# Chunk 1's token halves in a buffer of their own, and three engines' instruction order around the end of the front

## The reference

```
x = x + gated_delta(layernorm(x), Wq, Wk, Wv, Wo, Wb, bb, Wd, bd)
x = x + ffn(layernorm(x), w1, w2, w3)

gated_delta: q, k, v = x Wq, x Wk, x Wv;  beta = sigmoid(x Wb + bb);  delta = softplus(x Wd + bd)
             S_t = beta_t * S_{t-1} + delta_t * (k_t outer v_t);  o_t = q_t S_t;  out = o Wo
ffn:         quantize(w) = clip(round(w / (mean|w| + 1e-8)), -1, 1)
             (sigmoid(x q(w1)^T) * (x q(w2)^T)) q(w3)^T
```

## Time and profile before

| | us |
|---|---|
| median of 3 runs (341.34 to 343.6) | 341.43 |
| the profiled execution | 342.33 |
| its span, first to last instruction | 340.6 |
| TensorE busy in the span | 331.5 |
| VectorE, ScalarE, GpSimd busy | 205.7, 141.2, 102.0 |

### The profile page before, as it was taken

How to read it: one execution, slowest core, us unless ns; L and a number is a source line. 1 busy time by engine, 2 the same in 40 slices (tenths; PEclk the granted TensorE clock), 3 DMA queues, 4 the chain that set the end, 5 groups by cost and what they waited for, 6 DMA issues and landing times.

```text
span 340.6 us, 5194 instructions
## 1 busy us (share of the span) xinstructions
PE 331.5 (97%) x1824; PEld 184.4 (54%) x1824; DVE 205.7 (60%) x454; ACT 141.2 (41%) x270; POOL 102.0 (30%) x350
## 2 busy tenths in 40 slices
PE   8999999979999999999999999999999999999996
PEld 6888878864544544445455444454554444444442
DVE  3777999489978967276388652564886412343411
ACT  1588767789673663322324250223242102323200
POOL 5797645586001105990011044600110300000000
PEclk9999999999999999999999999999999999999999
DMA  7999700474572351400004022000030320000011
GB/s 204 365 387 403 280 0 2 92 95 94 102 115 47 50 106 41 115 32 2 0 0 64 0 70 86 31 1 3 0 62 2 73 81 33 0 0 3 0 62 62
DMA packets 45658, 26.94 MB, mean 79 GB/s; under 512 B 37568, under 2 KB 38080, under 8 KB 45632
## 3 DMA queue, kind: packets, MB, share of 16 engines
q1 hardware_dynamic: 45312, 26.62, 29.2%
q10 hardware_dynamic: 320, 0.00, 0.0%
HBM read 13.89 MB, written 4.19 MB: 53 GB/s over the span
## 4 chain that ended last, share of the span: by engine, by line
PE 83%; POOL 7%; DVE 4%; issue 3%; DMA 1%; ACT 1%; SPq 0%; POOLq 0%
PE ffn L1060 45%; PE ffn L1074 22%; PE lev L955 4%; PE lev L985 4%; PE ffn L924 2%; PE oc L971 2%; DMA w_nat<-xs 1%; POOL rs L377 1%; PE oc L968 1%; DVE X L742 1%; PE lev L974 1%; POOL xs L440 1%; PE oc L958 1%; DVE stats L680 1%; PE oc L960 1%
## 5 line engine op out<-in xcount | busy, mean ns | idle before, releaser
L1060 PE MATMUL ffn<-w_nat,w12T 128*128 128x512 f16 x704 | 155.3, 379 | 2.5 <-DMA w_nat<-xs 2.5
L1060 PEld LDWEIGHTS ffn<-w_nat,w12T 128*128 128x128 f16 x704 | 68.6, 98 | 84.6 <-issue 2.7
L1074 PE MATMUL ffn<-w3T,w_nat 128*128 128x512 f16 x352 | 76.6, 379 | 0.0
L644 ACT ACTIVATE xnT<-ffn 128x512 f32<-128x512 f32 x44 | 26.2, 596 | 99.4 <-PE ffn L1060 99.3
L871 DVE SCALAR_TENSOR_TENSOR xnT<-ffn,xnT 128x512 f32<-128x512 f32 x44 | 30.3, 689 | 57.1 <-PE ffn L1060 56.9
L1074 PEld LDWEIGHTS ffn<-w3T,w_nat 128*128 128x128 f16 x352 | 34.4, 98 | 42.6 <-ACT w_nat L650 1.0
L376 POOL TENSOR_TENSOR ve<-mv,rconst 128x2 f32<-128x2 f32 x16 | 3.3, 206 | 127.2 <-DVE mv L684 127.2
L885 DVE SCALAR_TENSOR_TENSOR x_sb<-ffn,x_sb 128x512 f32<-128x512 f32 x16 | 11.1, 691 | 43.1 <-PE ffn L1074 43.1
L876 DVE TENSOR_TENSOR w_nat<-xnT,w_nat 128x512 f16<-128x512 f32 x44 | 30.9, 701 | 0.4
L650 ACT ACTIVATE w_nat<-xnT 128x512 f16<-128x512 f32 x44 | 27.4, 623 | 6.5 <-DVE xnT L871 6.4
L680 DVE BATCH_NORM_STATS2 stats<-x_sb 128x6 f32<-128x512 f32 x32 | 20.5, 683 | 2.2 <-issue 1.8
(11 more groups left out here) (118 smaller groups left out, 375.5 us busy)
## 6 DMA issues: line engine op xcount, KB each, us to landing
x_sb<-in_L_attn_x_dram SPq DMA_DIRECT2D x16, 256.0 KB, 8.2
out_dram<-x_sb SPq DMA_DIRECT2D x16, 256.0 KB, 2.0
w_nat<-in_L_ffn_w_dram SPq DMA_DIRECT2D x2, 1536.0 KB, 12.5
w_nat<-in_L_ffn_w_dram SPq DMA_DIRECT2D x2, 1408.0 KB, 14.5
w_nat<-in_L_ffn_w_dram SPq DMA_DIRECT2D x2, 1280.0 KB, 13.3
wv<-in_L_attn_Wv_dram SPq DMA_DIRECT2D x1, 256.0 KB, 5.1
wo<-in_L_attn_Wo_dram SPq DMA_DIRECT2D x1, 256.0 KB, 12.9
w_nat<-xs SPq DMA_TRANSPOSE x16, 3.3
```

Source lines behind the costliest of these rows:

```text
L644: nc.scalar.activation(sig[:, u % 2, :], bank[2 * u % 3][:, :], ACT.Sigmoid, scale=1.0 / XS).then_inc(sig_ready, 1)
L1060: done = nc.tensor.matmul(bank[n % 3][:, :], w12T[:, a * DT + t, u * P:(u + 1) * P], xT[:, g, part, t, :], start=t == 0 and part == 0, sto ...
L1074: done = nc.tensor.matmul(bank[(2 * HT + m) % 3][:, :], hid[:, part, j, m * P:(m + 1) * P], w3T[:, j, :], start=part == 0 and j == 0, stop ...
```

## The change

Chunk 1, and every later odd chunk, writes its fp16 halves into `xs_odd`, which lies over slot 0 of `xn`. That slot is last read by the transposes of chunk 6 (`tile_T` 14), and its front part is used by `q3` in group 0. So the waits are altered: `xhi(1)` waits for `tile_T` 14 where it waited for chunk 0's transposes, chunks 2 and up wait for the transposes of chunk c-2, `sign3(0)` waits for chunk 1's transposes, and `xhi(3)` waits for all transposes of the third weight. Then instructions are moved:

- GpSimd: the mask of level 0 is made behind `fetch(0)` and no longer ahead of `gates(0)` (a new semaphore `masks_made` tells VectorE); `norm(4)` stands ahead of `gates(1)`; `xlo(0)` ahead of `norm2(1)`.
- ScalarE: `apply(6)` ahead of `xhi(0)`, `vcopy(5)` ahead of `sign12(0)`, and `xhi(1)` ahead of `apply(7)`.
- VectorE: `chain1(0)` ahead of `gates(1)`; `apply(6)` ahead of `steps(0)`; `round12(0)` behind `mean_var(7)` and `xlo(0)`; `round12(1)` behind `xlo(1)`; `steps(1)` in unit 1 of group 0 where it was in unit 2.
- TensorE: `spread(1)` after unit 0 of group 0, where it was after unit 1. Nothing else moves on TensorE. SP's order is as before.

```diff
+        xs_odd = xn[:, 0, :, :].rearrange("p b d -> p (b d)").bitcast(f16).rearrange("p (b s d) -> p b s d", b=B, s=2)
...
+        def halves(c):
+            return xs_odd if c % 2 else xs
...
-                    sp_.dma_start_transpose(xT_tile(c, b), xs[:, b, :, :].rearrange("p s n -> p (s n)")
+                    sp_.dma_start_transpose(xT_tile(c, b), halves(c)[:, b, :, :].rearrange("p s n -> p (s n)")
...
             def xlo(c):
-                if c > 0:
-                    pool.wait_ge(xT_in, 16 * B * c)
+                if c > 1:
+                    pool.wait_ge(xT_in, 16 * B * (c - 1))
                 pool.wait_ge(xhi_ready, B * c + 1)
-                nc.gpsimd.tensor_tensor(xs[:, 0, 1, :], xn2[:, 0, :], xs[:, 0, 0, :],
+                nc.gpsimd.tensor_tensor(halves(c)[:, 0, 1, :], xn2[:, 0, :], halves(c)[:, 0, 0, :],
...
-            make_masks(range(1))
             gates(0)
             fetch(0)
+            make_masks(range(1))
+            norm(4)
             gates(1)
-            norm(4)
             fetch(1)
             gates(2)
             norm(5)
             norm2(0)
             norm(6)
+            xlo(0)
             norm2(1)
-            xlo(0)
             norm(7)
             xlo(1)
...
             def sign3(j):
                 act.wait_ge(rounded3, DT if j < 5 else 2 * DT)
+                if j == 0:
+                    act.wait_ge(xT_in, 16 * B * 2)
...
                 if s == "xhi":
-                    if c > 0:
-                        act.wait_ge(xT_in, 16 * B * c)
+                    if c > 1:
+                        act.wait_ge(xT_in, 16 * B * (c - 1))
+                    if c == 1:
+                        act.wait_ge(tile_T, 2 * 7)
+                    if c == 3:
+                        for n in range(QS):
+                            act.wait_ge(w3_in[n], 16 * len(range(n, HT, QS)))
                     for b in range(B):
                         act.wait_ge(xn2_ready, B * c + b + 1)
-                        nc.scalar.activation(xs[:, b, 0, :], xn2[:, b, :], ACT.Copy).then_inc(xhi_ready, 1)
+                        nc.scalar.activation(halves(c)[:, b, 0, :], xn2[:, b, :], ACT.Copy).then_inc(xhi_ready, 1)
...
+            apply(6)
             attn("xhi", 0)
-            apply(6)
             zcopy(5)
             evacuate_T(6)
+            vcopy(5)
             sign12(0)
-            vcopy(5)
+            attn("xhi", 1)
             apply(7)
             zcopy(6)
             evacuate_T(7)
-            attn("xhi", 1)
             sign12(1)
...
             attn("chain0", 0)
+            attn("chain1", 0)
             gates(1)
-            attn("chain1", 0)
...
+            apply(6)
             steps(0)
-            apply(6)
             attn("norm2", 1)
-            round12(0)
             mean_var(7)
             attn("xlo", 0)
+            round12(0)
             attn("apply", 1)
-            round12(1)
             apply(7)
             attn("xlo", 1)
+            round12(1)
             gates(3)
...
-                        if u == 2:
+                        if u == 1:
                             steps(1)
...
-                    if g == 0 and u == 1:
+                    if g == 0 and u == 0:
                         spread(1)
```

More of the change, by code:

```diff
@@ L126, in build_gated_delta_ternary_ffn @@
         bias_in = sem("bias_in")
-        consts, filled = sem("consts"), sem("filled")
+        consts, filled, masks_made = sem("consts"), sem("filled"), sem("masks_made")
         resid_ready = sem("resid_ready")
@@ L369, in make_masks @@
                                                      pattern=[[-2 * h, n], [0, h]], channel_multiplier=1))
-                    nc.gpsimd.affine_select(out=m, in_=m, compare_op=ALU.is_gt, fill=0.0, base=h,
-                                            pattern=[[2 * h, n], [0, h]], channel_multiplier=-1)
+                    made = nc.gpsimd.affine_select(out=m, in_=m, compare_op=ALU.is_gt, fill=0.0, base=h,
+                                                   pattern=[[2 * h, n], [0, h]], channel_multiplier=-1)
+                made.then_inc(masks_made, 1)
             def rstd(c, n, mv, rs, scale, after=None):
@@ L761, in attn @@
                     dve.wait_ge(levels_done, c + 1)
-                    if c > 0:
+                    if c == 0:
+                        dve.wait_ge(masks_made, 3)
+                    else:
                         dve.wait_ge(o_done, c)
@@ L799, in attn @@
                 if s == "xlo":
-                    if c > 0:
-                        dve.wait_ge(xT_in, 16 * B * c)
+                    if c > 1:
+                        dve.wait_ge(xT_in, 16 * B * (c - 1))
                     dve.wait_ge(xhi_ready, B * c + 2)
-                    nc.vector.tensor_tensor(xs[:, 1, 1, :], xn2[:, 1, :], xs[:, 1, 0, :],
+                    nc.vector.tensor_tensor(halves(c)[:, 1, 1, :], xn2[:, 1, :], halves(c)[:, 1, 0, :],
                                             ALU.subtract).then_inc(xlo1_ready, 1)
```

## The result

The changed kernel takes 339.29 us (median of 7 runs, 339.15 to 339.53) against 341.48 for the kernel before beside it. The ratio on record is 0.992, with a 95% interval of 0.9896 to 0.9944. The medians differ by 2.2 us or 0.64%, where 3.3 us were forecast (338.1). It is inside the stated range of 337.6 to 340.2, and inside "within 1%", the likeliest case. Between the two profiled executions the span fell by 2.8 us, from 340.6 to 337.8. How 2.8 in the traces and 2.2 in the medians go together is the first thing the experiments had to settle.

A forecast was written before the change was run, and what follows sets the result against it. TensorE was taken as the bound, busy 331.5 of 340.6 us. Levels 0.73, chunk 7 0.0, group 0 2.53 and its start 0.0 gave 3.3 us: 338.1 from the 341.43 median, range 337.6 to 340.2.

The forecast's parts named there:

- within 1%: Outcome class for the whole kernel: time changes by no more than one per cent, 3.4 us; chance 0.60.
- three named waits of TensorE in the front: TensorE waits before chunk 0's levels (0.73), chunk 7's transposes (0.30) and group 0 (2.53), together 3.56 us.
- second rival: Chunk 7's transposes: `xhi(1)` holds `apply(7)` back, TensorE begins at 65.2 to 65.8; total 338.5 to 339.1; chance 0.13.
- Wait three: Before group 0, TensorE waits for chunk 1's transposed halves; all 2.53 us go, with 1.9 us to spare.
- Wait one: Before chunk 0's levels, TensorE waits for VectorE's chain; the wait goes whole, 0.73 us.
- I cost it at nothing: `norm(4)` ahead of `gates(1)` on GpSimd costs nothing; with `fetch(1)` late, at most 0.73 us would be lost.
- Wait two: Before chunk 7's transposes, TensorE's wait stays at about 0.3 us (0 to 0.5), starting at 64.8.
- The port rule: GpSimd and certain VectorE instructions exclude each other; TensorE would begin chunk 7's transposes at 65.0, sum 3.1 instead of 3.3.
- the quiet 4.67: GpSimd's two root chains before `norm(7)` ends: 4.67 us, costed from a chain in quieter company, against 5.46 before.
- The new buffer is what lets `xhi(1)` stand in front: ScalarE, before group 0: `xhi(1)` can move ahead because it no longer waits for chunk 0's halves to leave `xs`.
- the slower rival: Group 0: `spread(1)` stalls TensorE if `xlo(1)` ends after 67.1; later units lose 1.5 or more; 341.7 to 343; chance 0.05.

The follow-up runs named there:

- mask_early: The changed kernel with the level-0 mask made first of all on GpSimd, no longer behind `fetch(0)`; 339.05 us, ratio 0.9891.
- one_buffer: The changed kernel with all its orders, but every chunk's halves in `xs` again, with the waits of before; 339.32 us, ratio 0.99.
- move_one: The kernel before with only ScalarE's `xhi(1)` moved ahead of `apply(7)`, in the one buffer; 344.24 us, ratio 1.0054.
- chain_only: The kernel before with only the edits around chunk 0's chain (level-0 mask, `norm(4)`, `chain1(0)` ahead of `gates(1)`); 341.29 us, ratio 0.9971.
- xhi1_late: The changed kernel with ScalarE's `xhi(1)` back behind `apply(7)`, `zcopy(6)` and `evacuate_T(7)`; 342.94 us, ratio 1.0035.
- spread_late: The changed kernel with `spread(1)` after unit 1 and `steps(1)` in unit 2 again, as before; 339.38 us, ratio 0.9912.
- both: The changed kernel with the level-0 mask made first on GpSimd, and chunk 7's statistics, `norm(7)` and `apply(7)` moved forward; 338.79 us, ratio 0.9895.
- move_two: The kernel before with ScalarE's `xhi(1)` ahead of `apply(7)` and the second buffer with its waits; 339.75 us, ratio 0.9929.

## Why the prediction was right, and where its terms were off

The forecast's case came true: three named waits of TensorE in the front were the whole matter, nothing behind group 0's start moved (264.40 us both times), and no rival decided. (TensorE began chunk 7's transposes at 65.35, inside the 65.2 to 65.8 of the second rival, but `apply(7)` waited for `norm(7)` and not for `xhi(1)`, which ended at 63.75.) The size was over by 1.1 us, and these terms hold it:

- *Wait three, 2.53 us.* It went whole, but it was read from one execution that was 0.9 above the median. In the second profile it is 1.98. The text said that the profiled execution lay above the median and then carried the full 3.3 over to the median: that is the step that failed. Profile against profile, 339.0 was forecast and 339.53 came, and only 0.5 is missing. The mixing accounts for 0.55.
- *Wait one, 0.73 us.* It went whole as worked out, but its size too belonged to that execution: 0.41 in the second. It accounts for 0.32.
- *"I cost it at nothing; were `fetch(1)` late by it ..."* It was late, and 0.27 us stood before chunk 1's levels. The bound of 0.73 was sound, the value taken was not. I named `norm(4)` alone as a cause. The moved masks are enough for it (`mask_early`), and the 0.6 us that `norm(4)` took more at its new place may have a share. I had counted these masks' relief ahead of `gates(0)` and their cover as a finished product, but not that they still take 1.4 us of GpSimd ahead of `fetch(1)`.
- *Wait two, 0.3 (0 to 0.5).* It was 0.46, from the upper end: `norm(7)` ended at 64.46. The port rule that I set beside this spread would have put TensorE's start at 65.0 in place of 64.8, and it came at 65.35 with TensorE itself 0.4 late, mostly from the loss above. GpSimd's two chains took 5.54 us (58.92 to 64.46), so the row of before (5.46) was right and the quiet 4.67 was not to be had. One of its instructions, L382, took 1.54 us beside VectorE's `xlo(0)` and `round12(0)`, where the same instruction of the two chains took 0.82 and 0.69 in the kernel before. By this the trace agrees in kind with the Trainium skill (SBUF — State Buffer, section "SBUF: two separate sides") and its exclusive port pair. No run here isolates the port. This term accounts for 0.16.

These four terms (0.55, 0.32, 0.27 and 0.16) make 1.3, 0.2 more than is missing, and the rest is within what two profiles of one kernel differ by.

By the second profile of before, 0.41 + 0.30 + 1.98 = 2.69 us of waits were there, and 0.28 + 0.46 = 0.74 are left in the second profile of the changed kernel: 1.95, against 2.1 between the spans and 2.2 between the medians.

Two things that I argued were wrong or incomplete. "The new buffer is what lets `xhi(1)` stand in front" is refuted by `one_buffer`. My own working had `xlo(0)` done 3.3 us earlier, so that `xs` was free when `xhi(1)` came, and I did not draw that conclusion. And the slower rival had the right place and condition, and a term in its price (1.5 us in the later units) that did not come. It also lies one edit away and not in the change: with `xlo(1)` early, `spread(1)` never waits.

## What to carry to other kernels

When a wait on a DMA is the largest term, take its length from several executions, or subtract what the profiled one lies above the median before you carry the sum over. A long wait of TensorE can cost more than itself: look at the granted clock behind it, as in `move_one`. An edit that moves work on a half-idle engine need not be free behind the move: ask who reads the next product on that engine, and move it into a gap that the timeline shows, as the mask could be. And where a change adds a buffer and reorders, try each alone: a buffer frees a move only if its old wait would still be open at the new place.

## What the runs showed of the hardware

The landing of the second transpose took 5.0 and 4.4 us in the two profiles of the kernel before, against 3.2 to 3.4 in the changed one. The DMA view shows a hole in the traffic. The kernel before from 72 to 73 us, with an instruction fetch of 0.02 MB on queue 8 (packets, MB, then the queue's share), and from 73.3 to 74.3:

```profile
DMA packets 713, 0.19 MB, mean 191 GB/s; under 512 B 712, under 2 KB 712, under 8 KB 712
...
q8 instruction: 1, 0.02, 9.1%
```

```profile
DMA packets 17, 0.00 MB, mean 4 GB/s; under 512 B 17, under 2 KB 17, under 8 KB 17
```

713 packets in the first stretch, 17 in the second, with two transposes issued and not done. In the changed kernel, again from 72 to 73 us, the same fetch falls into a pause of the transposes, and nothing is held up:

```profile
DMA packets 1, 0.02 MB, mean 16 GB/s; under 512 B 0, under 2 KB 0, under 8 KB 0
...
q8 instruction: 1, 0.02, 8.6%
```

The fourteen profiles were compared. In eight, transposes were in flight at the fetch (the two of the kernel before, `chain_only`, `one_buffer`, `xhi1_late`, `mask_early`, `spread_late`, `both`), and in all eight the traffic all but stopped 0.5 to 1 us behind it, for 1 to 1.5 us. In the other six the fetch met no transposes or their last packets, and there is no hole to see. Only in the kernel before and in `chain_only` did the hole fall on chunk 1's halves and so on TensorE (in `chain_only` the second landed after 4.3 us). In the others it fell on a weight stripe that was not yet wanted. Transposes in flight alone do not do it: in `move_two` they follow one another from 65 to 70 us with no fetch, and no half microsecond there has fewer than 338 packets. That the fetch is the cause wasn't tried by itself and stays open, since no run moved the fetch alone. If it is, some 1.2 to 1.7 us of the old wait came from the moment of a fetch, and the change gained part of its time by issuing the transposes before that moment.

The second point is VectorE beside GpSimd. VectorE's `apply(7)` in `xhi1_late`, where GpSimd's `xlo(1)` does not run beside it:

```profile
64.42 0.55 DVE L707 TENSOR_SCALAR xn<-x_sb,mv,rs 128x512 f32<-128x512 f32 x1 [1.60 <-POOL shift L392]
```

In the changed kernel the same instruction took 1.36 us. GpSimd's 128x512 `xlo(1)` had started 0.08 us before it and ended at 65.57, and VectorE's ended 0.28 us after that, at 65.85. So it is in all fourteen profiles: in the seven in which `xlo(1)` starts just before it, it takes 1.36 us and ends 0.28 us behind `xlo(1)`, and in the seven others it takes 0.54 or 0.55. That is what one would see if VectorE stood still until GpSimd was done. It cost TensorE little: its eight transposes behind it, four of which read the result, took 1.20 us in place of 1.09 in `xhi1_late`.
